# Two sub-groups of each tail tile moved to the border of two steps, and the tail tile put ahead of the dense block, in the first layer of a graph network kernel

## The reference, cut to what matters

```python
dst = jnp.minimum((12500 * jax.random.uniform(k3, (400000,)) ** 2.0).astype(jnp.int32), 99999)
_o = jnp.argsort(dst, stable=True); src = src[_o]; dst = dst[_o]
...
h = jnp.maximum(_layernorm(x), 0.0)
# layer 0: norm = deg_inv[from] * deg_inv[to]
m_j = norm[:, None] * (x_j + x_j * x_i @ W1_w.T + W1_b)
x = x + leaky(segment_sum(m_j, to_))
h = jnp.maximum(_layernorm(x), 0.0)
# layers 1 and 2, twice:
mean_neigh = segment_sum(h[src], dst) / jnp.maximum(deg, 1.0)[:, None]
h = h @ W_self.T + mean_neigh @ W_neigh.T + b
```

## Time and profile before

| | |
|---|---|
| median of three runs | 4134.81 us |
| profiled execution | 4136.51 us, its span 4134.8 us |
| busy in the span | PE 3652.7 us (88%), POOL 2863.6 (69%), DVE 2021.7 (49%), ACT 1180.7 (29%) |
| chain that ended last | PE 49%, POOL 29%, issue 10%, DVE 6%, DMA 5% |
| step 3 to step 49 of layer 0 | 440 to 1854 us of the span |
| its last products | to 1891 us |
| first visit of steps 4, 22, 26, 34 and 49 | 479.8, 1047.7, 1164.7, 1393.9 and 1822.0 us |

### The profile page before, as it was taken

How to read it: one execution, slowest core, us unless ns; L and a number is a source line. 1 busy time by engine, 2 the same in 40 slices (tenths; PEclk the granted TensorE clock), 3 DMA queues, 4 the chain that set the end, 5 groups by cost and what they waited for, 6 DMA issues and landing times.

```text
span 4134.8 us, 67045 instructions
## 1 busy us (share of the span) xinstructions
PE 3652.7 (88%) x24703; PEld 2323.7 (56%) x24703; DVE 2021.7 (49%) x5265; ACT 1180.7 (29%) x3014; POOL 2863.6 (69%) x2906
## 2 busy tenths in 40 slices
PE   0028988899999999998999999999999999999999
PEld 0025666666666666665555555555655565666565
DVE  3589988877777777773232322323221222211311
ACT  0043555556666666651020110212100010100100
POOL 5502677777777777653777777777757777777775
PEclk9998999999999999999999999999999999999999
DMA  5172455556666666667667677676787767677675
GB/s 158 47 174 87 143 194 193 186 191 223 196 225 213 205 218 195 212 204 243 242 223 271 219 258 252 243 261 217 266 280 268 253 249 271 231 266 272 228 277 203
DMA packets 385930, 905.09 MB, mean 219 GB/s; under 512 B 74847, under 2 KB 319528, under 8 KB 365378
## 3 DMA queue, kind: packets, MB, share of 16 engines
q1 hardware_dynamic: 193377, 590.39, 38.5%
q0 software_dynamic: 134256, 278.85, 22.6%
q10 hardware_dynamic: 57968, 31.48, 2.8%
HBM read 662.42 MB, written 238.96 MB: 218 GB/s over the span
## 4 chain that ended last, share of the span: by engine, by line
PE 49%; POOL 29%; issue 10%; DVE 6%; DMA 5%; ACT 0%; DVEq 0%; POOLq 0%; ACTq 0%; SPq 0%
PE ps L1456 35%; POOL arena L1252 26%; PE ps L1367 6%; PE ps L1427 5%; DMA arena<-parts,arena 4%; POOL arena L1217 2%; DVE arena L1684 2%; DVE arena L1681 2%; PE ps L1404 1%; DMA table<-arena 1%; DMA arena<-in_dst 1%; DVE arena L1757 0%; PE ps L1382 0%; ACT arena L1127 0%; PE ps L1394 0%
## 5 line engine op out<-in xcount | busy, mean ns | idle before, releaser
L1252 POOL DMA_INDIRECT arena<-parts,arena x2690 | 2701.2, 1004 | 968.9 <-issue 805.2
L1456 PE MATMUL ps<-arena 128*128 128x384 bf16 (+1 forms) x15778 | 3040.0, 329 | 71.9 <-DVEq L1758 67.2
L1456 PEld LDWEIGHTS ps<-arena 128*128 128x128 bf16 x15778 | 1527.4, 98 | 984.4 <-ACT arena L1048 71.4
L1048 ACT ACTIVATE arena<-ps 128x392 bf16<-128x392 f32 x1824 | 899.6, 499 | 1361.6 <-PE ps L1427 1348.8
L1427 PE MATMUL ps<-arena 128*128 128x196 bf16 (+1 forms) x5102 | 1030.9, 239 | 100.4 <-DVE arena L1684 89.6
L1709 DVE TENSOR_TENSOR arena<-arena 128x640 bf16<-128x640 bf16 (+1 forms) x587 | 270.3, 464 | 1241.8 <-PE ps L1367 1240.6
L1427 PEld LDWEIGHTS ps<-arena 128*128 128x128 bf16 x5102 | 474.7, 101 | 311.0 <-DVE arena L1684 94.8
L1367 PE MATMUL ps<-arena 128*128 128x384 bf16 (+1 forms) x2690 | 542.6, 330 | 83.7 <-DMA arena<-parts,arena 83.4
L1681 DVE TENSOR_TENSOR arena<-arena 128x768 bf16<-128x768 bf16 (+3 forms) x881 | 475.3, 539 | 254.1 <-PE ps L1427 249.2
L1684 DVE TENSOR_TENSOR arena<-arena 128x1176 bf16<-128x1176 bf16 (+4 forms) x881 | 555.5, 631 | 0.0
L1367 PEld LDWEIGHTS ps<-arena 128*128 128x128 bf16 x2690 | 259.8, 98 | 267.1 <-issue 101.1
(11 more groups left out here) (155 smaller groups left out, 1181.1 us busy)
## 6 DMA issues: line engine op xcount, KB each, us to landing
arena<-counts SPq DMA_DIRECT2D x100, 3136.0 KB
counts<-arena SPq DMA_DIRECT2D x54, 3136.0 KB
arena<-parts,arena POOLq DMA_INDIRECT x2690
arena<-parts SPq DMA_DIRECT2D x28, 672.0 KB, 9.1
arena<-table SPq DMA_DIRECT2D x196, 64.0 KB
parts<-arena ACTq DMA_DIRECT2D x110, 96.0 KB
parts<-arena SPq DMA_DIRECT2D x14, 679.0 KB, 6.5
parts<-arena SPq DMA_DIRECT2D x86, 96.0 KB
```

Source lines behind the costliest of these rows:

```text
L1048: act.activation(stage[k][:, :, a - g * P:b - g * P], ps[:, unit_bank(q), 0:(b - a) * tiles].rearrange("p (n a) -> p a n", n=b - a), ACT.C ...
L1252: pool.indirect_dma_start(ring[:, m % RSUBS * CHUNKS + c, 0:W0 if nth == 0 else W1C], None, parts_of[nth], bass.IndirectOffsetOnAxis(ap=ta ...
L1456: m = pe.matmul(bank(b, 0, w), stage[k][:, a, :], Xp[:, a, 0:w], start=e == 0, stop=e == tiles - 1, skip_group_check=True)
```

## The change

It edits the order in which engines meet layer 0 only.

1. `tile_at`: in layer 0 the tail tile of a step comes ahead of the dense block in the order of tiles (`pair[::-1]`).
2. Sub-groups of a tail tile: the first two stand ahead of visits 1 and 3 of the step, the others at 0.3, 0.525 and 0.75 of it (0.3 and 0.75 where there are four). `ready` may come before the step (it was held to its first one-hot).
3. `take` of the tail tile stands at 0.85 of its own step, `take` of the dense block at the border as before; `tick` no longer takes tiles below position 2 * GROUPS, and one `take` stands ahead of the last stretch.
4. The semaphore `s_aggt` goes; `take` of a tail tile waits for `s_tail` at the count of its last sub-group.

```diff
-        tile_at = [t for s in range(steps) for t in (dense_at[nth][s], None if tail_at[nth][s] is None else GROUPS + tail_at[nth][s])]
+        pairs = [(dense_at[nth][s], None if tail_at[nth][s] is None else GROUPS + tail_at[nth][s]) for s in range(steps)]
+        tile_at = [t for pair in pairs for t in (pair if nth else pair[::-1])]
...
             for e, n in enumerate(due):
-                w = starts_at[g] + 14 + (visits_in[g] - 14) * e // len(due)
+                w = starts_at[g] + 1 + 2 * e if e < 2 else in_slot(g, 0.3 + 0.45 * (e - 2) / (len(due) - 3))
                 sub_after.setdefault(w, []).append(n)
-                ready_before.setdefault(hot_at(max(starts_at[g], w - 20)), []).append(n)
+                ready_before.setdefault(hot_at(max(starts_at[1], w - 20)), []).append(n)
                 gather_at.setdefault(max(starts_at[1], w - 40), []).append(n)
             for e in range(2):
-                take_before.setdefault(during(starts_at[g] + 2 + 5 * e), []).append(2 * s + e)
+                take_before.setdefault(during(starts_at[g] + 1 if e else in_slot(s, 0.85)), []).append(2 * s + e)
...
+        take_before.setdefault(during(in_slot(GROUPS - 1, 0.85)), []).append(2 * GROUPS - 2)
...
                 t.then_inc(s_tail, 1)
-                if first + count == tail_visits[subs[n][0]]:
-                    pe.sem_inc(s_aggt, 1)
...
-                    dve.wait_ge(s_aggt, tails_before[nth] + i + 1)
+                    dve.wait_ge(s_tail, subs_before[nth] + subs_of[t - GROUPS][-1] - first_sub[nth] + 1)
...
-                take(nth, j)
+                if nth or j >= 2 * GROUPS:
+                    take(nth, j)
...
                 for n in last_due:
                     ready(0, n)
+                take(0, 2 * GROUPS - 1)
```

More of the change, by code:

```diff
@@ L449, in program @@
         s_free = sem("s_free")
-        s_aggt = sem("s_aggt")
         s_freet = sem("s_freet")
```

## The result

The changed kernel took 4108.38 us, the median of four runs (4104.02 to 4112.94). The kernel before took 4138.99 us beside it, the median of four (4133.2 to 4146.87). The ratio is 0.9927, with a 95% interval of 0.9907 to 0.9947: faster by 0.7%. The sum of the prediction was -34.6 us. The medians are 30.6 us apart, and the two profiled spans, 4134.8 and 4102.3 us, 32.5.

| stretch of layer 0 | before, us | after, us | difference | forecast |
|---|---|---|---|---|
| up to step 4 | 479.8 | 481.1 | +1.3 | in the next |
| steps 4 to 21 | 567.9 | 565.4 | -2.5 | |
| steps 22 to 25 | 117.0 | 123.1 | +6.1 | |
| steps 26 to 33 | 229.2 | 229.3 | +0.1 | |
| up to step 34, together | 1393.9 | 1398.9 | +5.0 | -6 (-15 to +6) |

A forecast was written before the change was run, and what follows sets the result against it. POOL was taken to pace steps 4 to 21 and TensorE steps 34 to 48; -25.6 - 6 - 3 = -34.6 us of 4136.5 gave 4102, stated as 4101 for the median, range 4083 to 4125.

The forecast's parts named there:

- The border: Layer 0 step borders: two sub-groups fill the wait, saving 1.75 us at odd and 1.45 at even ones, mean 1.6.
- The check at odd borders: Profile after: first product 2.1 to 2.3 us behind the first visit at odd borders, no release wait there.
- Both signs of being wrong: Steps 34 to 48 staying over 28 us, or step 22 starting over 8 us off, less step 4's shift.
- GpSimd's room in steps 34 to 48: Steps 34 to 48: POOL at 1.379 us a gather can follow 26.9 us steps, with waits for TensorE near 10 us.
- Steps 4 to 33: Layer 0, steps 4 to 33 together: -6 us, with -15 and +6 as ends.
- rival 1: POOL paces all of layer 0, a gather costing 1.46 us instead of 1.38; -17 us, 4118, chance 0.15.
- Waits for gathers in steps 4 to 21: Steps 4 to 21: TensorE waits 50 us or over for gathers instead of 27.6, same length within 8 us.
- The last stretch: End of layer 0: the first product's 2.81 us release wait goes, saving 3 us.
- Rival 2: Layer 0 borders: VectorE comes 1.5 us later, a border gives 0.2 us; -5 us, 4130, chance 0.11.
- Rival 3: Steps 4 to 21: late landings at the border starve the ring, 17 steps 3 us longer; +22, 4157, chance 0.06.
- the -15 end: Steps 4 to 33 if a gather beside a store is hardly delayed: -15 us, the sum at 4093.
- rival 4: Steps 4 to 33: landings do not bite, POOL keeps its head start, -9 and -12 in full; -48, 4087, chance 0.10.

The follow-up runs named there:

- e1: Changed kernel with no sub-group at the border, the 4 or 5 of a step spread evenly from visit 14 to 0.75; 4144.74 us, ratio 1.0004.
- e2: Changed kernel with the third sub-group of a step at 0.42 of it instead of 0.3; 4127.8 us, ratio 0.9959.
- e3: Changed kernel with each store of a block of counts held until the next step's third sub-group is through; 4119.49 us, ratio 0.9947.
- e4: Changed kernel with every tail tile of layer 0 one step earlier and no sub-group in the last stretch; 4123.7 us, ratio 0.9953.
- e9: Changed kernel as it is, on a slower chip where the kernel before took 4942.27 us; 4874.9 us, ratio 0.9853.

## Why the prediction was right, and where it was not

**The border, right in both halves.** Forecast 1.75 us at odd and 1.45 at even borders. In steps 34 to 48 a tile has 19 or 18 gathers, and the two sub-groups at the border are nine matmuls, 9 x 0.165 = 1.49 us. Measured there: odd 2.35 + 1.49 - 1.99 = 1.85, even 2.56 + 1.49 - 2.57 = 1.48. Step by step it is the same: step 34, behind an even border, went from 28.46 to 26.97 us, and step 35, behind an odd one, from 28.49 to 26.65. Eight even and seven odd borders are 24.8 us, 1.65 each. The odd border was a little under-sized because I gave the six visits 0.6 us, and they take 0.5.

The step that the sum did not have is the clock. The other 1.6 us of the 26.4 all come from step 36, which took 30.13 us before and 26.97 after. Before, TensorE ran at its lower level there (granted clock 0.50 from 1453.95 to 1457.3 us), right behind a wait for the release of 1.67 us. e1, whose even borders still wait 1.66 us, has one such slow time in steps 34 to 48 too, in step 44. The changed kernel and e2, e3 and e4, whose borders are covered, have none there. So the 26.4 are 6.0 of order and take, 18.8 of sub-groups under the wait and 1.6 of clock. e1 shows that neither edit was a by-product of the other.

**The check at odd borders.** "2.1 to 2.3 us" held in steps 27 to 33 (2.16), not in 17 to 25 (1.83) or 35 to 49 (1.99). "2.6 to 2.8" at even ones was 2.57. Release waits under 5 us held in steps 34 to 48 (0.7) and not in steps 4 to 21 (9.1, of which more than half are pieces of 0.6 to 0.7 us up to step 12); none at odd borders holds from step 15 on. Both signs of being wrong stayed away: steps 34 to 48 took 26.8 us each, and step 22 began at 1046.5 us instead of 1047.7.

**GpSimd's room in steps 34 to 48, right that it can follow, wrong about what is left.** I expected waits near 10 us there and there are 0.9. Two errors add up. First, 1.379 us a gather took the whole 35.2 us off, but thirteen of those gaps hold 0.3 us of issue each, which stay: (392.9 + 3.9)/285 = 1.392. Second, a gather now lasts 306.60/284 = 1.080 us instead of 302.10/285 = 1.060, with VectorE at 333.81 of 401.7 us (83%) instead of 78%. That 0.020 is three times the 0.007 that I had from rows. That VectorE's share is the cause is not shown, and steps 22 to 33 speak against it: there VectorE was busy 78% before and 76% after, and a gather took 261.36/252 = 1.037 us before and 267.79/250 = 1.071 after. Together that is (401.7 - 0.9)/284 = 1.41, and the room that I had put at 10 us is used up.

**Steps 4 to 33, the term that was mis-sized.** Forecast -6, measured +5.0, inside the stated -15 to +6 and at its bad end. The direction of each part was right: GpSimd started sooner, at 441.78 instead of 447.75 us, and had 46 gathers out when step 4 began, where before it had 42. It could have been more: two gathers of 8.18 and 4.72 us came in between (before 3.91 and 4.65). The rest is a count. At the first visit of step 34 both kernels had issued 690 gathers: 648 in 914.1 us before (1.411 each), 644 in 917.8 after (1.425). So: +1.3 us at step 4, -5.6 for four gathers, +9.3 for 644 at 0.0145 more each, +5.0 together. I had a cost of 0.007 in the text and no time for it in the sum, and had hoped for 12 us from steps 22 to 33, in which GpSimd was already full in the earlier trace rows. There the kernel before waited for no gather, and the changed one waits 19.1 us in six pieces, in steps 22 to 33. TensorE stopped being the pace there and GpSimd became it, as rival 1 had it for all of layer 0, with the stands beside the store on top, as e3 shows.

**Waits for gathers in steps 4 to 21.** I expected 50 us or over, and they are 36.2. The length of the stretch was right within 2.5 us. The waits have an extra price that the sum did not hold, the clock: step 20 lost 6.5 us to a stand of 4.84. As I read it that does not lengthen the stretch while GpSimd is the pace; it makes TensorE's waits fewer than the missing time.

**The last stretch.** Forecast 1.6 + 3, measured 7.3. The 2.81 us wait of the earlier trace rows is gone, as said, and the border gives 1.8. Of the other 2.7 us some 2.3 are the clock, an estimate: at a granted clock of 0.50 TensorE was busy for 7.86 us of this stretch before (1853.3 to 1860.1, from that wait on, and 1887.4 to 1890.8) and for 3.34 us after (1855.6 to 1859.0), and half of the difference is 2.3. e1, without sub-groups at the border, already has 62.9 us there, so 6.2 of the 7.3 came with the order of tiles and takes.

**Layers 1 and 2** are 3.8 us shorter, where I had nothing. Two runs of one kernel differ by as much.

**The rivals.** Rival 2, VectorE late, did not happen: at the odd border shown its release is 0.8 us early (1.35 against 2.16), and at the even one TensorE waits 0.25 us for it. Rival 3, landings at the border, happened in e2 and e4 (stands of 10.19 and 9.50 us) and not in the changed kernel, whose longest stand is 4.8 us. I had put its condition at GpSimd's waits for the ring. The traces say otherwise: GpSimd never stops for the ring in e2 either (396 gaps of 0.3 us of issue), and what decides, as far as e2 and e3 show, is which sub-group's gathers are out as the store begins. The stand was 10.19 us in e2, and in e3, where the store was held back, no stand in steps 22 to 33 was over 2.3. The Trainium skill, "DMA: Bandwidth & Descriptors", section on queues, rings and completion order, says that a DMA engine takes turns between its queues packet by packet. That a gather beside a store would be late by little more than its own length was my step from there, and it needs short packets. In e2 the store's transfers of 25 KB had 4 us to themselves while gathers were out. How many of them make one packet the trace does not tell, so the runs refute my step and leave the rule of the Trainium skill open.

**Slips in the sum.** 4136.5 - 34.6 - 1.7 is 4100, not 4101; the sum at the -15 end is 4091, not 4093; and rival 4 adds up to -50 and 4085, not -48 and 4087. None moves the range.

**What stays open.** That GpSimd's pace hides the gain in steps 4 to 33 rests on counts (it never stops there, 1.41 to 1.43 us a gather) and on e3, whose waits add up to the same 55 us, not on a run that gave GpSimd room, since the runs meant for it fell on the slow chips. Why a gather takes 1.093 us in e1 and 1.052 in e4 over the same steps is not known either.

## What to carry to other kernels

A wait that comes back at every border of a loop can be filled with work that is already in the program, if that work's own inputs are ready there: here two sub-groups hid 1.0 to 1.5 us each time (18.8 us in 15 borders), moving the releasing operation forward brought 6.0 more, and the clock, which no longer fell behind the waits, 1.6. Before the gain is multiplied by the number of borders, count for each stretch what the next engine issues in it, with its stands taken out in full: where that engine is already full, the gain is zero, and a longer operation of it (0.0145 us on 644 gathers) turns it negative. A late input should not be moved about without a look at what its neighbours will catch: the stand of 4.8 us in the middle of a step became one of 10.2 us at the border.

## What the runs showed of the hardware that was not expected

- Behind a stand of TensorE of 4.84 us matmuls took twice their time for some 3.4 us. A short wait can do it too: in the kernel before, the 15 release waits of 1.2 to 1.7 us in steps 34 to 48 were followed by such a slow time once, in step 36. Stands up to 2.3 us were followed by none in steps 22 to 33 of e3, where the granted clock stayed at 1.00.
- A gather issued across the start of the 3136 KB store landed up to 8 us after its issue: the last of a sub-group was issued by 547.9 us, and TensorE had the sub-group at 555.77 (e2). For 4 us of that, 547 to 551, only the store's transfers began.
- Single gathers held GpSimd for 8.92 and 4.91 us near 450 us (e4), and for 8.18 and 4.72 us at 444.48 and 455.55 in the changed kernel, where most take 0.95 to 1.1; the kernel before has 3.91 and 4.65 at 458.17 and 463.71, e2 one of 13.34 at 451.91. In e1, e2, e3 and e4 steps 4 to 21 had means of 1.093, 1.086, 1.061 and 1.052 us, for the same work in another order.
- On the slower chips TensorE, VectorE and ScalarE stood together for 4 to 6 us again and again: in e9 ScalarE came back at 1669.31 us, VectorE at 1669.31 and TensorE at 1669.86. Leaving out 214 gathers, for which nobody waited, made the kernel 239 us faster there (4874.9 to 4636.19). What the engines stand for the profile does not name; that it grows with the transfers under way is what these runs suggest, and no run isolates it.
